# Attention: stores of q and k by whole batch, two stacks loaded in the core, heads and sums fetched through ScalarE's queue

## The reference

```
q, k, v = x @ Wq + bq, x @ Wk + bk, x @ Wv + bv     # 16 heads of 8 channels
scores  = einsum('bhqd,bhkd->bhqk', q, k) * scale    # causal
w       = softmax(scores)
x       = x + (einsum('bhqk,bhkd->bqhd', w, v) @ Wo + bo)   # x: layer norm of the residual
```

## Time and profile before

| | |
|---|---|
| time, median of 3 runs | 5766.71 us (5761.96 to 5769.86) |
| the profiled execution | 5796.54 us, its span 5794.8 us |
| TensorE busy | 4718.3 us, 81% |
| VectorE busy | 3782.7 us, 65% |
| ScalarE busy | 3159.8 us, 55% |
| GpSimd busy | 1685.3 us, 29% |
| mean granted TensorE clock | 0.92 |
| projection ends, core starts in layers 2, 4, 6, 8, 14 | 888.46, 1657.58, 2381.55, 3098.94, 5018.29 us |

### The profile page before, as it was taken

How to read it: one execution, slowest core, us unless ns; L and a number is a source line. 1 busy time by engine, 2 the same in 40 slices (tenths; PEclk the granted TensorE clock), 3 DMA queues, 4 the chain that set the end, 5 groups by cost and what they waited for, 6 DMA issues and landing times. The chain is left out here.

```text
span 5794.8 us, 91401 instructions
## 1 busy us (share of the span) xinstructions
PE 4718.3 (81%) x33501; PEld 2088.3 (36%) x33596; DVE 3782.7 (65%) x4596; ACT 3159.8 (55%) x6002; POOL 1685.3 (29%) x1468
## 2 busy tenths in 40 slices
PE   5677667998679977799766998589877799699999
PEld 2233223443233335333352333256432344233344
DVE  6899657886589943899437992577638710699410
ACT  5666444676448852488524885434466521388621
POOL 0666315885032324322242221000006400123100
PEclk7899888999889988899887999789989999799999
DMA  0000011111021124211242110000000000111100
GB/s 27 0 1 1 4 42 41 42 44 28 10 71 51 51 86 148 71 50 51 83 142 73 49 50 20 6 10 2 5 10 0 20 0 0 37 31 45 42 0 14
DMA packets 132106, 211.55 MB, mean 37 GB/s; under 512 B 36422, under 2 KB 93619, under 8 KB 130293
## 3 DMA queue, kind: packets, MB, share of 16 engines
q1 hardware_dynamic: 126708, 197.74, 11.3%
q0 software_dynamic: 4992, 8.41, 0.5%
HBM read 153.93 MB, written 52.00 MB: 36 GB/s over the span
## 5 line engine op out<-in xcount | busy, mean ns | idle before, releaser
L947 ACT ACTIVATE l_core_probs<-l_core_ps_scores_b 128x512 f32<-128x512 f32 (+3 forms) x3840 | 1610.7, 508 | 581.0 <-PE l_core_ps_scores_b L863 426.2
L1047 DVE TENSOR_REDUCE l_core_chunk_max<-l_core_ps_scores_a 128x2 f32<-128x1024 f32 (+3 forms) x1280 | 1253.7, 1021 | 82.9 <-PE l_core_ps_scores_a L848 47.8
L863 PE MATMUL l_core_ps_scores_b<-l_q_rows_sb,l_k_rows_sb 64*128 64x512 bf16 (+3 forms) x3840 | 944.0, 332 | 32.5 <-ACT l_core_probs L947 10.1
L848 PE MATMUL l_core_ps_scores_a<-l_k_rows_sb,l_q_rows_sb 64*128 64x512 bf16 (+3 forms) x3840 | 741.4, 346 | 163.9 <-DVE l_core_ps_acc L1005 75.9
L996 POOL TENSOR_SCALAR_AFFINE_SELECT l_core_probs<-l_core_probs 128x512 f32<-128x512 f32 x512 | 326.9, 639 | 1169.9 <-ACT l_core_probs L947 1165.7
L878 PE MATMUL l_core_ps_acc<-l_core_probs,l_v 128*9 128x512 f32 (+3 forms) x6144 | 648.9, 494 | 15.9 <-ACT l_core_out_sums L929 9.1
L1047 DVE TENSOR_REDUCE l_core_neg_max<-l_core_ps_scores_a 128x2 f32<-128x256 f32 (+3 forms) x640 | 493.6, 820 | 97.6 <-PE l_core_ps_scores_a L808 96.0
L863 PEld LDWEIGHTS l_core_ps_scores_b<-l_q_rows_sb,l_k_rows_sb 64*128 64x128 bf16 x3840 | 304.4, 94 | 689.9 <-ACT l_core_probs L947 600.4
L1918 POOL TENSOR_TENSOR l_scan_bx<-l_xs,l_scan_b_rows 128x1024 f32<-128x1024 f32 x192 | 452.5, 2357 | 224.1 <-DVE l_scan_states L1928 217.8
L1928 DVE TENSOR_TENSOR_SCAN l_scan_states<-l_scan_ps_decay,l_scan_bx 128x1024 f32<-128x1024 f32 x192 | 439.8, 2290 | 40.7 <-POOL l_scan_bx L1918 15.3
L966 POOL TENSOR_TENSOR l_core_probs_decayed<-l_core_probs,l_decay 128x1536 f32<-128x1536 f32 (+2 forms) x160 | 394.2, 2488 | 156.5 <-ACT l_core_probs L947 156.5
(11 more groups left out here) (323 smaller groups left out, 7683.4 us busy)
## 6 DMA issues: line engine op xcount, KB each, us to landing
l_slots_weights<-m_both_dram SPq DMA_DIRECT2D x78, 512.0 KB
l_q_rows<-l_proj_parts SPq DMA_DIRECT2D x96, 128.0 KB
l_k_rows<-l_proj_parts SPq DMA_DIRECT2D x96, 128.0 KB
l_q_rows_sb<-l_q_rows SPq DMA_DIRECT2D x128, 96.0 KB
l_k_rows_sb<-l_k_rows SPq DMA_DIRECT2D x128, 96.0 KB
l_heads_out<-l_core_out_sums SPq DMA_DIRECT2D x300, 32.0 KB
l_q_rows_sb<-l_q_rows SPq DMA_DIRECT2D x128, 64.0 KB
l_k_rows_sb<-l_k_rows SPq DMA_DIRECT2D x128, 64.0 KB
```

Of the source, the lines that this page charges most:

```text
L848: mm = nc.tensor.matmul(slot[:, i, 0:w], qs[n % 3][rows, p, qt * P:(qt + 1) * P], ks[n % 3][rows, p, c * NT:c * NT + w], start=True, stop= ...
L863: mm = nc.tensor.matmul(pb[m % 3][:, 0:w], ks[n % 3][rows, p, kt * P:(kt + 1) * P], qs[n % 3][rows, p, q0:q0 + w], start=True, stop=not diag)
L947: nc.scalar.activation(pt[:, ts % RP, j, 0:w], pb[m % 3][:, 0:w], ACT.Exp, scale=scale).then_inc(b_free, 1)
L1047: nc.vector.tensor_reduce(to, pa[e % 2][:, :, 0:width_a(qt, c)], AX.X, ALU.max, negate=True).then_inc(a_free, 1)
```

## The change

Stores of q and k: batches 0, 1 and 2 are stored whole, 6 DMAs of 1024 tokens in place of 12 of 512; batch 3 stays in halves. Only stack 0 is loaded in the projection, after batch 1. Stacks 1 and 2 are loaded at the start of the core, ahead of the first maxima. `heads_back` of the first three batches moves from SyncE, at the end of groups 6, 10 and 14, to ScalarE, inside the same groups after the exponentials of their seventh step. There ScalarE also waits for the stores of the batch's heads and for the store of the inverted sums. The wait before stack 0 and the last one count fewer DMAs.

```
--- before.py
+++ after.py
@@ -511,21 +511,25 @@
                 sp.wait_ge(rows_clear, 6)
                 load_consts_(sp)
-                for b in range(B):
-                    for h in range(2):
-                        sp.wait_ge(hi, 4 * b + 2 * h + 2)
-                        sp.wait_ge(mid, 4 * b + 2 * h + 2)
-                        sp.wait_ge(low, 4 * b + 2 * h + 2)
-                        for j, n in enumerate("qk"):
-                            for s_ in range(3):
-                                sp.dma_start(parts[n][s_, b * R:(b + 1) * R, h * NT:(h + 1) * NT],
-                                             part[0:R, j, s_, b * S + h * NT:b * S + (h + 1) * NT]
-                                             ).then_inc(stored if b else first_stored, 16)
-                    if b == 1:
-                        sp.wait_ge(first_stored, 16 * 12)
-                    if b in (1, 2):
-                        load_stack(sp, b - 1)
-                sp.wait_ge(stored, 16 * 12 * (B - 1))
+                def store(b, h, width, sem_):
+                    at = b * S + h * NT
+                    done = 4 * b + 2 * h + width // NT * 2
+                    sp.wait_ge(hi, done)
+                    sp.wait_ge(mid, done)
+                    sp.wait_ge(low, done)
+                    for j, n in enumerate("qk"):
+                        for s_ in range(3):
+                            sp.dma_start(parts[n][s_, b * R:(b + 1) * R, h * NT:h * NT + width],
+                                         part[0:R, j, s_, at:at + width]).then_inc(sem_, 16)
+
+                store(0, 0, S, first_stored)
+                store(1, 0, S, stored)
+                sp.wait_ge(first_stored, 16 * 6)
+                load_stack(sp, 0)
+                store(2, 0, S, stored)
+                store(3, 0, NT, stored)
+                store(3, 1, NT, stored)
+                sp.wait_ge(stored, 16 * 24)
@@ -764,13 +768,14 @@
-                def heads_back(b, h):
+                def last_heads_back(b, h):
...
+                load_stack(sp, 1)
                 load_stack(sp, 2)
                 max_rows(0)
...
-                    if n >= 4 and n % 4 == 2:
-                        heads_back(n // 4 - 1, HEADS)
...
@@ -935,6 +938,14 @@
+                def heads_back(b):
+                    for u in range(2):
+                        act.wait_ge(o_stored[u], 128 * (2 * b + 2))
+                    act.dma_start(o[:, b, :], heads_out[b * P:(b + 1) * P, :]).then_inc(r_in[b], 16)
+                    act.wait_ge(r_out[b], 16)
+                    src = rsums[b * HEADS:(b + 1) * HEADS, :].rearrange("(h o) t -> h o t", o=1)
+                    act.dma_start(r[:, b, :], src.to_broadcast((HEADS, P // HEADS, S))).then_inc(r_in[b], 16)
+
...
+                    if ts % (4 * NS_) == 2 * NS_ + 6 and ts > 4 * NS_:
+                        heads_back(ts // (4 * NS_) - 1)
```

More of the change, by code:

```diff
@@ L799, in _ @@
                 inverse_rows(B - 1, 12)
-                heads_back(B - 1, 12)
+                last_heads_back(B - 1, 12)
             @block.tensor
```

## The result

The changed kernel takes 5714.10 us (median of 4 runs, 5710.86 to 5715.77) beside 5768.28 us of the kernel before (median of 4): a ratio of 0.9907, interval 0.9890 to 0.9924, faster by 54 us. The forecast was 5716. A later set of runs gave 0.9909 (0.9894 to 0.9924).

What follows compares the result with a forecast made beforehand. Score loops were taken as engine-bound, with SyncE's issue queue last at the projection's end. Projection -52.5, core start +2, stalls -12.7 and ScalarE +13 gave -50 us, from 5766.71 to 5716; range 5700 to 5739.

Steps and rivals of the forecast that it cites:

- Projection, -52.5: End of the projection in five attention layers: fewer SyncE issues save 11.5, 11.5, 8.5, 7.0 and 14.0 us; ends 39 and 58.
- the queue's account: End of the projection: SyncE's queue of issues is last, so issues taken away shorten it; 14.0 us in layer 14.
- three groups of six issues of 3.0 give 870.4; plus the tail of 6.5: Projection of layers 2 and 8: from 861.44, core starts at 877.0 instead of 888.46, 11.5 us each.
- Whole-batch stores cost the same per issue: Projection stores with 2 KB per partition: same time per issue as half-batch stores; upper bound double.
- Rival 3: Projection: whole-batch stores take double per issue, so the queue isn't shortened by them; -41 us, 5725; 5%.
- Start of the core, +2: Start of the cores: first row of maxima queues behind stacks 1 and 2, 1 us late in layer 2; 2 us for all.
- Stalls go, -12.7: Core, layers 4, 6 and 8: loads issued after the stack has landed remove the stretched distances' excess, 12.7 us.
- ScalarE pays 13: Core: 30 issues on ScalarE cost 9 us and waits for the inverse sums' store 4 us, together 13.
- nine such stretched distances: Core, layers 4, 6 and 8: nine distances between rows of maxima stretched across heads loads, 12.7 us excess together.
- Rival 2: Core: loads meet the end of a stack, stalls of 12.7 stay, ScalarE pays 14.3 in full; -36 us, 5731; 17%.
- Rival 1: Core: ScalarE's issues are hidden and the stalls go; -63 us, 5703; 18%.
- Rival 4: Core: ScalarE waits for the inverse sums' store at all 15 places; slower, 5793 with 5 us each; 4%.

Runs made afterwards that it cites:

- stores alone: Kernel before with only q and k of batches 0 to 2 stored by whole batch; stack 1 still loaded in the projection, heads and sums on SyncE: 1.0004.
- stack 1 alone: Kernel before with only stack 1 loaded at the start of the core, ahead of stack 2; stores by half batch, heads on SyncE: 0.9924.
- cut stacks, heads on SyncE in the old place: Kernel before with whole-batch stores, stack 1 in the core and stack copies cut to one DMA per slot; heads on SyncE right behind stack n + 3: 0.9874.
- with cut stacks: Kernel after with the stacks' copies cut to one DMA for each slot, heads and inverse sums still on ScalarE's queue: 0.9879.
- heads alone: Kernel before with only heads and inverse sums of batches 0 to 2 fetched through ScalarE's queue at the seventh step: 0.9996.
- the last version: Kernel after with heads fetched by SyncE at a group's start, stacks cut to one DMA per slot, batch 3's six k stores on ScalarE's queue: 0.9859 to before.
- heads on SyncE, early: Kernel after with heads and inverse sums fetched by SyncE at a group's start, ahead of the maxima and stack n + 3: 0.9881 to before.

## Why the prediction was right, and where it was right for the wrong reason

- **Projection, -52.5: measured -55.2** (12.1, 8.7, 8.0, 12.3, 14.1 for 11.5, 8.5, 7.0, 11.5, 14.0). Right in each layer. In layer 14 the queue's account is the true one: stores alone gave 3.8 for 3.7, stack 1 alone 10.0 for 9.3, and there the tail was 2.4 throughout. In layers 4 and 6 VectorE is last, as I had it, and the move of stack 1 alone reaches it (8.6 and 8.4).
- **Layers 2 and 8 came out by another way.** The step "three groups of six issues of 3.0 give 870.4; plus the tail of 6.5" kept the tail as a constant. It isn't one: by the account above it is what the lowest engines have left, and in layer 2 it was 6.5 us with two stacks, 4.8 after and 3.3 with stack 1 alone. The queue got to 872.60, later than 870.4 (0.85 us because batch 2 started later in this execution, the rest since issues of the stores took up to 1.98 us for three), and the tail shrank. Both accounts give some 11 us (one stack is 13 us of bytes on its engines by that estimate, against 11 us of queue that the change takes away), so that the number came out here is luck. Only the parts told them apart: I would have given 3 us in layer 2 to the stores alone, and they brought 0.9. The prediction had the bytes on the few engines in view, kept them as a fixed tail of 6.5, and so charged the wrong resource.
- **Whole-batch stores cost the same per issue**: right; 1.78 and 1.88 us for three in layer 14 as before, 1.33 for the first three in layer 2. Rival 3 fell.
- **Start of the core, +2: measured 0.** The first maxima stand 26.5 to 27.3 us after the start in both. The queue behind two stacks didn't hold that row; by the same sum of bytes, two stacks take 26 us, and the row comes at 26.5, so it was close.
- **Stalls go, -12.7, and ScalarE pays 13:** the stalls of 8.6 us did go, and the cores came out 3.4 us longer in one profiled execution (0.6 in the other). The two sizes were about right. Cores that have neither (cut stacks, heads on SyncE in the old place) took 2284.4 us, so the stalls cost 12.4 us before, and ScalarE's way 15.8 and 13.0 after; with cut stacks it cost 6.5. The prediction's "nine such stretched distances" are eight in the trace; the 12.7 us are the excess of those eight. The split of ScalarE's price was wrong: the issues cost 0.35 us in the first two places of layer 14, where nothing is waited for, and by those 6.5 us 0.4 on average, not 0.6 (0.9 in layer 14's third place, where the second issue took 1.35 us), and the wait for the inverse sums' store cost 0.7 to 1.4 us in six places, not 0.7. Rival 2, the collision moves instead of going, is thus partly what happened: ScalarE now waited for a small store behind the same stack for which TensorE had waited, and heads alone gained nothing (0.9996). Its full price (5731) didn't come.
- **Rival 1** (the issues are hidden, 5703) fell: the distances across the first two places are 25.2 to 25.9 us in layers 4, 6 and 8 and 24.6 in layer 14, where 24.2 is undisturbed, and heads alone brought nothing.
- **Rival 4** (every place waits 5 us) fell: nine of fifteen places have 0.04 us between the two issues.
- Two slips that moved nothing: the sum of the upper bounds of the projection is 59.5, not 58, and SyncE's order in the projection is 12 stores, 14 loads, 18 stores, not 18, 14, 12.

What stays open: why two parts without attention take 176 or 190 us from one chip to another, and what lengthens SyncE's issues behind a stack. I tried nothing there. Cores of equal kernels differ by some 3 us from one execution to the next (2300.2 and 2297.4 for the kernel after), so smaller differences of cores prove nothing.

## What to carry to other kernels

When the DMA share sits at 1/16 or 2/16 while something waits, ask which copies have 2 or 3 as their outermost size; add up the bytes per DMA engine, not only issues per queue, and cut those copies so that they spread: here it cost some 0.9 us of queue a stack and was worth 27.6 us on the kernel before. Where the queue itself ends a stage, as in layer 14, that cost is paid in full. A DMA that is small can wait long behind such a copy, and moving its issue to another engine's queue moves the wait along. Two accounts of one wait that give the same number for the whole change are told apart by making its parts one at a time.

## What the runs showed of the hardware

- Issue time does not follow the bytes of a DMA. A stack's copies, with rows of 4 KB, took 0.29 us for 8 rows, 0.62 for 16 and 0.72 for 24. A store of q took 0.43 us for 128 rows, and one of 64 rows in layer 14 took 0.60 us, each with rows of 1 KB and of 2 KB alike. So it does not follow the rows alone either. The Trainium skill (DMA: Bandwidth & Descriptors, "Rules for kernel authors") says that spreading DMAs over issuing engines brings no bandwidth and saves sequencer issue time alone; the last version agrees: 3.5 us less in layer 14, nothing in layer 2, where the DMA share is 1.0.
- Issues on SyncE got longer in the stretch where, by the sum of bytes, the lowest DMA engines were behind: 2.42 us for three stores instead of 1.4, with stores alone in layer 2. What holds them was not tried by itself.
- ScalarE issues the heads' load in 0.33 us. SyncE takes 0.36 to 0.46 us right behind a stack, and 0.34 at a group's start (heads on SyncE, early): what stands ahead in the queue makes more of a difference than the engine.
